# A pair's attention transpositions and context product one pair later, in one PSUM bank

## The reference

```python
x = x + adjacency_layer(ctx, layernorm(x))       # scores of ctx, top 76 of 256 per row, sigmoid, symmetrised
x = x + mx_ffn(layernorm(x))                     # gate/up/down, 1024 wide, blocks quantised to fp8
x = x + latent_attention(layernorm(x), ctx)      # the layer that the change touches
x = x + top1_experts(layernorm(x))               # 32 masked ternary experts, router, top 1
```

```python
scores = einsum('bhsr,bhlr->bhsl', q_r, k_r)
attn = softmax(scores, axis=-1)
ctx_c = einsum('bhsl,bld->bhsd', attn, kv_r)     # the "context product"
ctx_lat = einsum('bhsd,hkd->bhsk', ctx_c, w_kc_kv)
return ctx_lat.transpose(0, 2, 1, 3).reshape(B, S, H * K) @ Wo.T
```

## Time and profile before

| | us |
|---|---|
| median of 3 runs | 658.96 (657.79 to 659.67) |
| the profiled execution | 655.62 |
| its span, from the first instruction to the last | 653.8 |
| PE busy | 540.6 (83%) |
| DVE busy | 411.6 (63%) |
| POOL busy | 307.6 (47%) |
| ACT busy | 248.4 (38%) |
| mean granted clock of PE, 1.00 being 2.4 GHz | 0.957 |

### The profile page before, as it was taken

The page is one execution under the profiler, slowest core; times in us unless marked ns, Lnnn a source line. Parts: engine busy times, 40 slices in busy tenths (PEclk is TensorE's granted clock), DMA queues, the critical chain, the costliest instruction groups (busy, mean ns, idle before and its releaser), DMA issues.

```text
span 653.8 us, 8556 instructions
## 1 busy us (share of the span) xinstructions
PE 540.6 (83%) x3032; PEld 339.6 (52%) x3032; DVE 411.6 (63%) x806; ACT 248.4 (38%) x674; POOL 307.6 (47%) x300
## 2 busy tenths in 40 slices
PE   2862676868797679899999899999997999999696
PEld 1752334545454557555555575555554766554442
DVE  3999793479667536976864569768644353534244
ACT  1842221232433223543344334433442245354143
POOL 3765344259739713263345532542455224345466
PEclk9985898899999799999999998999998999999799
DMA  7940100012202200000000000000000000000000
GB/s 288 408 146 14 51 0 5 1 65 97 97 33 97 90 0 21 1 5 1 2 1 1 17 1 2 1 2 1 0 1 1 17 2 2 1 1 1 17 1 16
DMA packets 10201, 24.56 MB, mean 38 GB/s; under 512 B 4464, under 2 KB 6512, under 8 KB 9264
## 3 DMA queue, kind: packets, MB, share of 16 engines
q1 hardware_dynamic: 9920, 23.24, 9.9%
q0 software_dynamic: 240, 0.79, 0.3%
HBM read 22.97 MB, written 1.05 MB: 37 GB/s over the span
## 4 chain that ended last, share of the span: by engine, by line
PE 52%; DVE 27%; POOL 7%; ACT 6%; issue 6%; DMA 1%; SPq 0%; POOLq 0%; DVEq 0%; ACTq 0%
PE s L512 13%; PE qc L512 11%; PE ga L512 10%; PE qb L512 10%; PE ua L512 6%; DVE wk L1062 4%; DVE top L1060 3%; PE tp L515 2%; ACT reg L857 2%; DVE amax L987 2%; DVE reg L1134 2%; POOL reg L1375 2%; DVE nmax L1141 2%; POOL wE L1421 1%; DVE masks L1212 1%
## 5 line engine op out<-in xcount | busy, mean ns | idle before, releaser
L1375 POOL TENSOR_TENSOR reg<-reg,rsum 128x512 f32<-128x512 f32 x64 | 68.3, 1089 | 129.7 <-DVE rsum L1148 129.7
L857 ACT ACTIVATE reg<-s,nmax 128x256 f32<-128x256 f32 x128 | 59.0, 476 | 45.8 <-DVE nmax L1141 45.8
L1212 DVE SCALAR_TENSOR_TENSOR masks<-s,route,masks 128x256 f32<-128x256 f32 x120 | 51.5, 477 | 38.5 <-PE s L512 38.3
L512 PE MATMUL s<-wE,xhi 128*128 128x512 fp8e4 x192 | 73.6, 383 | 1.3 <-ACT reg L857 0.9
L512 PE MATMUL s<-wE,xlo 128*128 128x512 fp8e4 x192 | 73.5, 383 | 0.0
L512 PE MATMUL qc<-reg,wM 128*64 128x256 f32 (+1 forms) x384 | 68.6, 396 | 2.8 <-DVE reg L1134 2.8
L515 PE MATMUL tp<-idn,reg 128*128 128x128 f32 x248 | 39.8, 283 | 31.8 <-POOL reg L1375 16.0
L512 PE MATMUL qb<-reg,wA_hi 128*128 128x256 f16 x384 | 64.6, 278 | 1.5 <-ACT reg L842 1.4
L779 ACT COPY reg<-tp 128x512 f32<-128x512 f32 (+1 forms) x56 | 32.0, 572 | 67.8 <-PE tp L515 67.8
L1141 DVE TENSOR_REDUCE nmax<-s 128x2 f32<-128x512 f32 x64 | 40.9, 680 | 22.7 <-PE s L512 22.7
L512 PEld LDWEIGHTS qc<-reg,wM 128*64 128x64 f32 (+1 forms) x384 | 37.2, 153 | 31.6 <-issue 21.8
(11 more groups left out here) (192 smaller groups left out, 1094.6 us busy)
## 6 DMA issues: line engine op xcount, KB each, us to landing
masks<-in_moe_masks SPq DMA_DIRECT2D x16, 512.0 KB, 3.3
wM<-in_att_wq SPq DMA_DIRECT2D x1, 2048.0 KB, 7.7
wE<-in_wo_t SPq DMA_DIRECT2D x1, 2048.0 KB, 11.2
reg<-in_kc_q SPq DMA_DIRECT2D x1, 1536.0 KB, 10.9
reg<-in_qr_t SPq DMA_DIRECT2D x1, 1536.0 KB, 18.3
xb<-in_x SPq DMA_DIRECT2D x4, 256.0 KB, 3.4
wU<-in_gate_w SPq DMA_DIRECT2D x1, 1024.0 KB, 12.9
wD<-in_up_w SPq DMA_DIRECT2D x1, 1024.0 KB, 14.9
```

Source lines behind the costliest of these rows:

```text
L512: return nc.tensor.matmul(dst, lhsT, rhs, start=start, stop=stop, skip_group_check=not check)
L857: nc.scalar.activation(attn[p % 2][:, k * S:(k + 1) * S], s.tensor[:, (k % 2) * S:(k % 2 + 1) * S], ACT.Exp, bias=nmax[:, o:o + 1], accum_ ...
L1212: ins = nc.vector.scalar_tensor_tensor(acc[:, t, chain], src, w, acc[:, t, chain], ALU.mult, ALU.add)
L1375: nc.gpsimd.tensor_tensor(a, a, rsum[:, o + 2 * hh:o + 2 * hh + 2].unsqueeze(2).to_broadcast([P, 2, S]), ALU.mult).then_inc(attn_ready.sem, 1)
```

## The change

In the order of PE, `attn_turn(b, p, 0)` moves behind all of pair p's iteration, straight ahead of `scores(b, p + 1)`, and `attn_turn(b, p, 1)` straight behind `scores(b, p + 1)`. `context(b, p)` stays in iteration p + 1 but moves behind `to_keys`. For pair 7 the three steps go into the next batch: around its first `to_keys` and behind `project_first(b, 1)`. All three now write bank TP; before, some second halves wrote UA, and `context` wrote QB. ACT's queue follows: it copies both transposed halves of pair p - 1 ahead of `softmax(b, p)`, and the context product behind the copy of `to_keys`. POOL's and the other waits on QB for `context` become waits on TP. No computation is added or left out.

```diff
@@ tensor_order
-        steps += [("to_keys", b, 0), ("project_first", b, 1), ("project", b, 1)]
+        if b >= 1:
+            steps += [("attn_turn", b - 1, PAIRS - 1, 0)]
+        steps += [("to_keys", b, 0)]
+        if b >= 1:
+            steps += [("attn_turn", b - 1, PAIRS - 1, 1)]
+        steps += [("project_first", b, 1)]
+        if b >= 1:
+            steps += [("context", b - 1, PAIRS - 1)]
+        steps += [("project", b, 1)]
         if b >= 1:
             steps += [("att_out", b - 1)]
         for p in range(PAIRS):
             first, second = BESIDE[min(b, 1)][p] if more else ([], [])
+            if p >= 1:
+                steps += [("attn_turn", b, p - 1, 0)]
             steps += [("scores", b, p)]
             if p >= 1:
-                steps += [("context", b, p - 1)]
+                steps += [("attn_turn", b, p - 1, 1)]
             if p + 1 < PAIRS:
                 steps += [("to_keys", b, p + 1)]
+            if p >= 1:
+                steps += [("context", b, p - 1)]
             if p + 2 < PAIRS:
                 steps += [("project_first", b, p + 2)]
...
-            steps += [("attn_turn", b, p, 0)]
...
-            steps += [("attn_turn", b, p, 1)]
         if b >= 1:
             steps += [("expert", b - 1, FILLS - 2)]
-        steps += [("context", b, PAIRS - 1)]
+    steps += [("attn_turn", B - 1, PAIRS - 1, 0), ("attn_turn", B - 1, PAIRS - 1, 1), ("context", B - 1, PAIRS - 1)]
@@ banks_of
-    if name == "attn_turn" and args[2] == 1 and args[1] < 4 and args[0] < B - 1:
-        return ["UA"]
...
-        "project": ["QB"], "to_keys": ["QC"], "scores": ["S0", "S1"], "attn_turn": ["TP"], "context": ["QB"],
+        "project": ["QB"], "to_keys": ["QC"], "scores": ["S0", "S1"], "attn_turn": ["TP"], "context": ["TP"],
@@ scalar
                 if more:
                     adjacency(b + 1)
+                if b >= 1:
+                    attn_turn(b - 1, PAIRS - 1, 0)
                 to_keys(b, 0)
+                if b >= 1:
+                    attn_turn(b - 1, PAIRS - 1, 1)
+                    context(b - 1, PAIRS - 1)
                 if more:
                     adjacency_tanh(b + 1)
...
                     if p >= 1:
-                        context(b, p - 1)
+                        attn_turn(b, p - 1, 0)
+                        attn_turn(b, p - 1, 1)
                     softmax(b, p)
                     if p == 0 and b >= 1:
                         moe_norm(b - 1)
                     if p + 1 < PAIRS:
                         to_keys(b, p + 1)
+                    if p >= 1:
+                        context(b, p - 1)
```

More of the change, by code:

```diff
@@ L726, in context @@
                     pe.wait_ge(k.drained, k.done(("attn_turn", b, p, hh)))
-                pe.wait_ge(QB.drained, QB.free(("context", b, p)))
+                pe.wait_ge(TP.drained, TP.free(("context", b, p)))
                 for hh in range(2):
                     for c in range(T):
-                        last = mm(QB.tensor[DC * hh:DC * (hh + 1), 0:S], kvn[:, c * 2 * DC:c * 2 * DC + DC],
+                        last = mm(TP.tensor[DC * hh:DC * (hh + 1), 0:S], kvn[:, c * 2 * DC:c * 2 * DC + DC],
                                   attT[:, (2 * hh + c) * S:(2 * hh + c + 1) * S], c == 0, c == T - 1)
-                last.then_inc(QB.filled, 1)
+                last.then_inc(TP.filled, 1)
             def att_out(b):
-                pe.wait_ge(QB.drained, QB.done(("context", b, PAIRS - 1)))
+                pe.wait_ge(TP.drained, TP.done(("context", b, PAIRS - 1)))
                 pe.wait_ge(QC.drained, QC.free(("att_out", b)))
@@ L863, in context @@
                     act.wait_ge(QC.filled, QC.done(("att_out", b - 1)))
-                drain(QB, ("context", b, p), cT[:, p * S:(p + 1) * S], QB.tensor[:, 0:S])
+                drain(TP, ("context", b, p), cT[:, p * S:(p + 1) * S], TP.tensor[:, 0:S])
             def moe_turn(b):
@@ L960, in _ @@
                     experts_of(experts[p][1])
-                    attn_turn(b, p, 0)
                     experts_of(experts[p][2])
@@ L966, in _ @@
                     experts_of(experts[p][3])
-                    attn_turn(b, p, 1)
                     if p == 0 and b >= 1:
                         route_exp(b - 1)
-                context(b, PAIRS - 1)
+            for hh in range(2):
+                attn_turn(B - 1, PAIRS - 1, hh)
+            context(B - 1, PAIRS - 1)
             expert(B - 2, FILLS // T - 1)
@@ L1364, in keys @@
                 if b >= 2:
-                    pool.wait_ge(QB.filled, QB.done(("context", b - 2, PAIRS - 1)))
+                    pool.wait_ge(TP.filled, TP.done(("context", b - 2, PAIRS - 1)))
                 k4 = kvns[b % 2].rearrange("p (t u d) -> p t u d", t=T, u=2)
```

## The result

The changed kernel takes 671.98 us in the median (four runs, 665.43 to 673.30) against 658.90: +13.1 us, ratio 1.018 with an interval of 1.011 to 1.025. Slower, as forecast (669.4, range 662.5 to 673). The profiled execution of after has a span of 669.6 us and took 671.38; that of before 653.8 and 655.62. The two are 15.8 apart, more than the medians, because before's profiled execution was one of its quick ones.

The account below looks back on a forecast made before the run. PE bounds most of the kernel, but DVE, POOL and mask DMA bound batch 0 and DVE the stretch behind att_out. -0.8 + 1.3 + 2 x (2.2 + 0.9) + 1.8 + 1.9 = +10.4 us: 669.4, range 662.5 to 673.

Parts of the forecast that it names:

- Batch 0, pair 4, -0.8: Batch 0: pair 4's gate matmuls no longer stand behind the first transposition and its POOL wait, 0.8 us earlier.
- Boundary, +2.2, +2.2, +1.8: Behind x_turn, pair 7's three moved steps delay att_out: +2.2 us each in batches 1 and 2, +1.8 in batch 3.
- The 0.3 for T1's copy: At the boundary, the context product waits 0.3 us until the second transposition is copied out of the shared bank.
- Clock at the boundary, +1.3 at the first, 0 at the second: Longer idle before x_turn: about 4.1 us lowers the clock, +1.3 us; 2.9 us at the next boundary costs 0.
- rival (d): Clock falls at the second boundary too, as batch 2 begins: +1.4 us, 670.8; chance 0.18.
- Middle, +0.9 each: Batches 1 and 2, middle: fills at pairs 3 and 5 +0.5 us, pair 6 +0.4, pair 7 0; +0.9 each.
- The loss at pairs 6 and 7 with `ffn_down`: Batches 1 and 2: pair 6 +0.4 us; pair 7's later fill +0.4, transposition gone from before ffn_down -0.4.
- Adjacent fills: Batches 1 and 2, pairs 3 and 5: expert fills on S0/S1 become adjacent, 0.27 us bare, twice: +0.5 us.
- Batch 3, +1.9: Batch 3: pair 0 -0.1 us, pair 4's wait for a fill's drain +0.4, pair 7's bank waits +1.6; sum +1.9.
- (a): PE's POOL waits are the path, all 16.0 us would go: 650.8 us, or 654.2 for the median; chance 0.13.
- (b): PE's slack in the DVE-bound stretch takes the boundary: 2 x 2.2 and 1.3 us vanish, 663.7; chance 0.12.
- (c): The shared bank costs at every pair, ACT late by 0.3 us in 28 pairs: +7 us, 676; chance 0.07.

Follow-up runs that it names:

- right half of the table: DVE start times compared between the changed kernel and the kernel before, both with idle transpositions keeping the clock up; medians 657.01 and 651.96 us.
- treated kernel before: Kernel before plus idle transpositions where PE waits long, 40 of them in free bank UA ahead of hidden_turn(1, 1): 651.96 us, ratio 0.991.
- treated changed kernel: Changed kernel plus idle transpositions where PE waits long, 40 of them in free bank UA ahead of hidden_turn(1, 1): 657.01 us, ratio 0.999.
- left half: DVE start times compared between the changed kernel and the kernel before, without idle transpositions; medians 671.98 and 658.90 us.

## Why the prediction was right or wrong

The verdict was right, the time was 2.6 us off, and the mechanism of the boundary held. But the total is nearer than its parts, and that is luck: the moved work and its waits were forecast at 9.1 us and measured at 5.5 (right half of the table, -0.69 to +4.80), 3.6 too much; the clock was forecast at 1.3 and is 8 in the medians, 6.7 too little.

- *Batch 0, pair 4, -0.8.* Measured -0.76. In the right half the same place gives -2.46: in the treated kernel before, T0's wait for POOL there (2.12 us) was followed by a clock of 0.79 over 8 us, and the first gate and up matmuls took 3.07 and 2.43 us, in the treated changed kernel 1.98 and 1.88. The other waits gave nothing, by the chain and by the kernel without any wait for POOL.
- *Boundary, +2.2, +2.2, +1.8.* Measured +2.18, +2.18, +1.79, and passed on whole. In the right half batch 3's is 0.22 only: from `x_turn` to the second rotation the treated kernel before takes 10.50 us at a clock of 0.84 and the changed one 10.71 at 1.00, so a clock gain hides the rest. The 0.3 for T1's copy is in it: the last matmuls of `project_first` start at 385.26 and the first of C at 385.76.
- *Clock at the boundary, +1.3 at the first, 0 at the second.* Measured +1.20 and +2.68. This is the step that failed. I read "after 3.08 us of idle time four matmuls took 1.98" as a rule and took 2.88 us for harmless; rival (d) had the event with 0.18 and 1.4 us. A wait's length alone did not decide it: behind 3.08 us before had the full clock at 199 (1.00 over 7 us), the kernel with the shared bank alone had 0.76 at the same place behind 3.07. And behind the unchanged wait of 1.55 us ahead of `x_turn`, before has 1.00 in batch 2 and 0.70 in batch 3 (from 496.7 to 500), and the kernel with pairs 0 to 6 alone 0.79 in batch 2, which cost it 1.70 us. So how much of the 2.68 every execution of the changed kernel pays, one profile can't say; the 8 us of the medians do not rest on it.
- *Clock at `adjacency_turn` and at 199, not in the sum.* 0.88 and 1.23 us in the table, where -0.45 stands at full clock, so 1.3 and 1.7; and 1.69 at 199. I had costed the vanished POOL waits of the DVE-bound stretch at nothing, and did not ask where PE would wait in their place. It was at `adjacency_turn`, 1.9 us long, and behind it the clock was at 0.76 in both batches, as in the kernel without POOL's waits. With pairs 0 to 6 alone it fell behind this wait in batch 1 (+1.23) and not in batch 2 (-0.44), with 1.92 us of waiting both times.
- *Middle, +0.9 each.* Between the fifth rotation and the hidden quantisation the treated pair gains 0.8 us and between that and `x_turn` it loses 0.92; the stretch before gives 0.38 and 0.19. Sum -0.26 and -0.06. The loss at pairs 6 and 7 with `ffn_down` was forecast at 0.4 and is 0.9; the gains I had not seen. One has a row: at 279.05 of the treated kernel before DVE waited 0.42 us for a fill that T0 stood ahead of, and in the treated changed kernel it does not wait there. Adjacent fills were forecast to cost 0.5, and nothing of that shows.
- *Batch 3, +1.9.* -0.42 up to pair 7's rotation and +1.17 from there to `att_out` (pair 7's three steps in one bank): 0.8 in place of 1.9.
- *Rivals.* (a) refuted by the kernel without POOL's waits. (b) refuted, 2.14 in and 2.14 out. (c) refuted: 8 waits instead of one per pair, and C's own bank would have cost 27 us. (d) true, at 2.68 us and not 1.4, and only one of eight clock steps in the left half.

Do the parts add up? In the left half the clock steps (1.90, 1.69, 0.54, 1.20, 1.33, 2.68, 1.67, 0.46) sum to 11.5 us, and the shift over the program is 17.0, which leaves 5.5. The right half has 5.5, with clock steps of both signs left in it (-1.6 at pair 4, +1.7 at the second `ffn_down` of batch 0, -1.6 at the start of batch 3, +1.4 behind the last `att_out`), which sum to nothing. And at one mean clock, 0.947, after's quickest run took 665.43 us and three runs of before 657.93 to 658.73: 7 us apart; after's other three ran at 0.930 to 0.935. The 0.54, at the second `ffn_down` of batch 0, I count as clock (0.68 in before and 0.55 in after over 222 to 232), but how it divides between clock and copies was not measured. The changed kernel itself has four runs only, so its 13.1 us is less sure than the rest.

## What to carry to other kernels

Before removing a wait, find who is late behind it: here 16 us of waits were worth nothing that could be measured, since in batch 0 DVE, POOL and the mask DMA set the time and in the DVE-bound stretch DVE does. Count what a moved step delays ahead of the next engine-bound stretch (that arrived whole, to a few hundredths of a us), and count the idle time it leaves behind: here waits of PE that grew by 1.3 to 1.4 us were followed by 1.3 to 2.7 us of slower matmuls in the profile. A bank belongs to whoever copies it out: look where that copy stands in its queue before giving a step a bank of its own, or a shared one.

## What the runs showed of the hardware that was not expected

- The clock fell behind idle times as short as 1.55 us (0.70 from 496.7 to 500 in before), 1.91 us (0.76 over the next 7 us) and 2.88 us (0.76 over 8), in stages where PE had been busy before, and stayed at 1.00 behind others of the same length. The Trainium skill (TensorE: Matmul & The Clock Gate, "HAM oscillation — how this bites in real kernels") tells of a kernel in which every wait makes the next burst begin at half clock; this case agrees that waits do it, but not behind every one, and its waits are shorter than the work between them.
- One kernel's executions differ by it. In the experiments before ran 66 times between 653.64 us (mean clock 0.957) and 662.20 (0.936), and the quicker ones are, with few exceptions, those with the higher clock (correlation -0.91). A profile is one draw: the same 4.49 us wait before `x_turn(0)` was followed by 6.9 us from the first rotation to the second in before, 8.5 in after and 10.7 in the kernel with pair 7 alone.
- Matmuls that nobody reads pay for themselves. The kernel before with 138 idle transpositions takes 651.22 us, 7.5 under itself and quicker than both kernels of the change; PE's busy time rises by 14.5 us and the whole time falls. It needs a bank that is free at once: fillers that had to wait for a copy cost about 5 us.
